# Expert rows added to the token rows in memory by accumulating scatters, and the last norm added to x1 in the output by accumulating stores

## The chip, the cores and the metric

The kernel runs on one core of one Trainium2 chip. The metric is device time in microseconds (us); lower is better. The core has a matrix engine (TensorE, PE in the profile), a vector engine (VectorE, DVE), a scalar engine (ScalarE, ACT), a general engine (GpSimd, POOL) and a synchronising engine (SyncE, SP), each with an instruction stream of its own that runs strictly in order. SP and POOL issue nearly all transfers of this kernel. The transfers themselves run on 16 DMA engines, which all queues share. What SP issues shows up in the profile as queue q1 (hardware_dynamic), what POOL issues as queue q0 (software_dynamic).

## What is computed

A residual block of attention and a residual block of a feed-forward layer, each between two layer norms. 4096 tokens of 512 numbers, in float32. The feed-forward layer has one shared expert for all tokens and eight experts of which each token uses two.

```
def _moe_forward(hidden_states, ...):
    x = hidden_states.reshape(-1, h)
    shared = jnp.einsum('ti,hi->th', jax.nn.silu(x @ sh_gate_w.T) * (x @ sh_up_w.T), sh_down_w)
    probs = jax.nn.softmax((x @ router_weight.T).astype(jnp.float32), axis=-1)
    top_v, top_i = jax.lax.top_k(probs, TOP_K)
    top_v = top_v / top_v.sum(axis=-1, keepdims=True)
    combine = (jax.nn.one_hot(top_i, E, dtype=top_v.dtype) * top_v[..., None]).sum(axis=1)
    out = jnp.zeros_like(x)
    for e in range(E):
        gu = x @ gate_up_proj[e].T
        gate, up = (gu[:, :I_MOE], gu[:, I_MOE:])
        cur = jax.nn.silu(gate) * up @ down_proj[e].T
        out = out + cur * combine[:, e:e + 1]
    return out + jax.nn.sigmoid(x @ shared_gate_w.T) * shared
...
x = x + _layernorm(_L0_attn_ref(_layernorm(x, axis=-1), ...), axis=-1)
x = x + _layernorm(_L0_ffn_ref(_layernorm(x, axis=-1), ...), axis=-1)
```

The x after the first of the last two lines is called x1 below.

## The kernel before

Tokens go in 8 batches of 512 (4 chunks of 128 rows; 32 chunks in all). `schedule()` writes out one list of pieces by hand, and every engine runs those pieces of the list that it has a part in, in the order of the list. So the list sets what is queued behind what on each engine. Every product is made of three matrix instructions (high and low halves of both factors; `three`, lines 690 to 692).

There are three stages.

1. **Attention, with the shared expert of batches 0 to 6 between its pieces** (0 to about 1495 us). It computes x1, stores it to `x1_scratch` (piece `x1o`), routes the tokens and scatters each token's normed row to two places in `x1_normed_by_expert`, where rows stand sorted by expert in pages of 256 (piece `sc`, 8 indirect transfers per batch; it is filled with zeros first by piece `zf`, 13 transfers in the first batch). The shared expert's weights come in halves of 128x768 into three buffers `ffn_w_raw` (piece `raw`, L643), and its result, times its gate, goes to `shared_scratch` (piece `sho`).
2. **The experts** (1495 to about 2008 us). 39 pages of two halves, so 78 steps of 128 rows. In step j POOL fetches the page's weights by an indirect load (`rgu`, L572, 128x2816 numbers, two buffers; `rdn`, L579, 128x1536, one buffer), ACT and DVE split them into high and low parts (`WG`, `WD`), PE computes, ACT copies the result to `moe_y` (L1032) and SP stores it to `expert_out` (piece `yo`, L666).
3. **The end** (2008 us on). PE runs the shared expert for batch 7: 11 tiles (76 < n < 88) of 36 matrix instructions, 24 for gate and up and 12 for down. Beside it, chunk by chunk, the final sum and norm run: SP loads x1 and the shared rows (piece `fl`, L675 and L677, 8 buffers), POOL gathers the token's two expert rows from `expert_out` (L591), DVE adds them by weight (L1317, two per chunk) and takes statistics (`FA`, L1320), DVE computes the norm's factors for four chunks (`FR`, a chain of 12 small operations), ACT shifts x1 and DVE adds the normed row (`FX`, L1039 and L1333), and SP stores the output (piece `fo`, L681). The load for chunk q+8 waits until the store of chunk q has landed (line 674), because it uses the same buffer.

In stage 3 the gate of tile n+1 waits on PE for the DVE product of tile n (`SI`, L1282) and for the split weights of its own tile (`SPL`, L1272 and L1275); the down product waits for `HL` (L1285).

Of the kernel before, what the change touches and what calls it, by code (L numbers as in the profile page):

```python
# [50 lines left out]
XG = 3  # L51
FS = 8
# [116 lines left out]
def moe_step(j):  # L169
# [36 lines left out]
def final_chunk(q):  # L206
    return [("FX", q), ("fo", q)] + ([("fl", q + FS)] if q + FS < NCH else [])

# [9 lines left out]
def schedule():  # L218
# [21 lines left out]
    for n in range(INTERLEAVED, F_MOE):  # L240
# [6 lines left out]
        if k == 8:  # L247
            parts[2] += [("XT", 0), ("xg", 3), ("rgu", 2)]
# [10 lines left out]
    for q in range(FS):  # L259
        seq += [("fl", q)]  # L260
    tiles = NF - F_MOE
    early = BEFORE * NC
# [5 lines left out]
    done_ = 0  # L268
    span = 3 * tiles - 6
    for i in range(3 * tiles):  # L270
        n = F_MOE + i // 3
        for p in ffn_parts(n)[i % 3]:
            if p[0] == "EV":
                seq += queue_rest(queue, done_)
                done_ = len(queue)
                seq += [("EV", *p[1:]), ("FA", NC * p[1] + p[2])]
                if p[2] == NC - 1:
                    seq += [("FR", p[1])]
                    for c in range(NC):
                        seq += final_chunk(NC * p[1] + c)  # L280
            elif p[0] != "sho":
                seq += [p]
        upto = min(len(queue), (i + 1) * len(queue) // (NT * 3 - 3))
        for p in queue[done_:upto]:
            seq += p
        done_ = max(done_, upto)
    for p in ffn_last(NF - 1):
        if p[0] == "EV":
            seq += [p, ("FA", NC * p[1] + p[2])]
# [6 lines left out]

def queue_rest(queue, done_):
    return [p for ps in queue[done_:] for p in ps]
# [44 lines left out]
def build(nc, x, w_att, w_ffn, w_gu, w_dn, w_router, b_qk, b_v, b_out, t_mask, t_dq, t_dk, t_lam, t_blk, t_ident,  # L344
          t_rank, t_newton, t_route, out):
    x_d = x.rearrange("(b c p) d -> b c p d", b=NB, c=NC)
    out_d = out.rearrange("(n p) d -> n p d", p=P)
    x1_d = nc.dram_tensor("x1_scratch", [NCH, P, D], F32, kind="Internal").ap()
    xt_d = nc.dram_tensor("xt_scratch", [NB, 2, P, KT * TOK], F32, kind="Internal").ap()
    sh_d = nc.dram_tensor("shared_scratch", [NCH, P, D], F32, kind="Internal").ap()  # L350
# [1154 lines left out]
```

## Time and profile before

| | us |
|---|---|
| Median of three runs (2217.8 to 2221.76) | 2218.04 |
| The profiled execution, its own time | 2218.5 |
| Its span in the trace | 2216.5 |
| PE busy | 2000.0 |
| DVE busy | 1272.7 |
| ACT busy | 962.8 |
| POOL busy | 266.5 |
| DMA, mean over the span | 188 GB/s |

The profiled execution is 2.0 us longer than its span, and 0.5 us above the median. PE is busy for 90% of the span, but this share is not the same in all stages. The page's 40 slices show tenths of a slice of 55 us: PE stands at 9 from slice 4 to slice 36 and at 6, 5, 6 and 4 in the last four, and the clock granted to PE is 9 (nine tenths or more) through all of the middle and 8, 7, 8 and 7 in the last four. Those four slices are stage 3. The names that the trace prints drop digits: `x_scratch` is `x1_scratch`, `fin_x` is `fin_x1`, `x_normed_by_expert` is `x1_normed_by_expert`.

### The profile page before, as it was taken

The page shows a single profiled execution, that of the slowest core. Times are in us where ns is not written, and L with a number is a line of the kernel's source. Part 1 is how long each engine was busy: PE and PEld are TensorE (multiplying, and loading weights), DVE is VectorE, ACT ScalarE, POOL GpSimd, SP SyncE. Part 2 cuts the span into 40 slices and gives each one's busy share as a digit, 9 for nine tenths or more (in the row PEclk, how much of TensorE's full clock was granted, in tenths as well). Part 3 has the DMA queues.
Part 4 walks back from the last instruction along what each step waited for, and adds up shares of the span by engine and source line. Part 5 has one row for each costly group of instructions (what it writes and reads, how often), then busy time and mean ns, then how long its engine had stood idle before and what let it go on. Part 6 is the DMA issues. An engine that isn't in the chain of part 4 may idle for free.

```text
span 2216.5 us, 28811 instructions
## 1 busy us (share of the span) xinstructions
PE 2000.0 (90%) x10192; PEld 1602.9 (72%) x10192; DVE 1272.7 (57%) x2960; ACT 962.8 (43%) x1946; POOL 266.5 (12%) x310
## 2 busy tenths in 40 slices
PE   6787999999999999999999999999999999996564
PEld 4465677777677776776777677779999999995443
DVE  3545564655555655655755554446666666665676
ACT  4333343433443443443443343346666666662222
POOL 1101001001001001001001002011111111115330
PEclk9898999999999999999999999999999999998787
DMA  7966245454355256254454347357777777757773
GB/s 246 399 218 214 60 146 194 141 169 162 107 171 179 69 182 205 69 186 144 134 190 133 103 137 247 108 194 239 245 247 244 242 243 245 252 186 256 233 261 125
DMA packets 153663, 416.85 MB, mean 188 GB/s; under 512 B 18401, under 2 KB 18545, under 8 KB 146353
## 3 DMA queue, kind: packets, MB, share of 16 engines
q1 hardware_dynamic: 118656, 239.13, 33.7%
q0 software_dynamic: 34432, 175.80, 22.0%
q8 instruction: 83, 1.36, 0.3%
q14 instruction: 60, 0.48, 0.1%
q10 hardware_dynamic: 432, 0.07, 0.0%
HBM read 307.98 MB, written 106.95 MB: 187 GB/s over the span
## 4 chain that ended last, share of the span: by engine, by line
PE 76%; DVE 11%; DMA 6%; issue 3%; ACT 2%; SPq 1%; POOL 0%; DVEq 0%; ACTq 0%
PE banks L690 21%; PE banks L692 20%; PE banks L691 20%; PE banks L753 4%; DMA xT_lo<-xt_scratch 2%; DMA out<-fin_x 2%; PE banks L761 2%; PE banks L765 2%; PE banks L865 2%; DVE fin_shared L1317 1%; PE banks L771 1%; DMA ffn_w_raw<-w_ffn 1%; PE banks L871 1%; PE banks L719 1%; DVE pair_stats L1079 1%
## 5 line engine op out<-in xcount | busy, mean ns | idle before, releaser
L690 PE MATMUL banks<-xT_hi,ffn_gate_up_hi 128*128 128x512 f32 x704 | 307.4, 437 | 73.1 <-DVE hidden_late L1282 40.6
L691 PE MATMUL banks<-xT_lo,ffn_gate_up_hi 128*128 128x512 f32 x704 | 284.8, 404 | 0.0
L692 PE MATMUL banks<-xT_hi,ffn_gate_up_lo 128*128 128x512 f32 x704 | 284.7, 404 | 0.0
L690 PEld LDWEIGHTS banks<-xT_hi,ffn_gate_up_hi 128*128 128x128 f32 x704 | 138.4, 197 | 126.4 <-DVE hidden_late L1282 53.5
L690 PE MATMUL banks<-moe_gu_hi,moe_xT_hi 128*128 128x352 f32 x624 | 215.7, 346 | 3.4 <-DVE moe_xT_lo L1299 3.4
L940 ACT COPY q_one_head<-qT 32x128 f32<-32x128 f32 x512 | 151.1, 295 | 117.8 <-PE banks L753 112.5
L692 PE MATMUL banks<-moe_gu_hi,moe_xT_lo 128*128 128x352 f32 x624 | 201.8, 323 | 0.0
L691 PE MATMUL banks<-moe_gu_lo,moe_xT_hi 128*128 128x352 f32 x624 | 201.3, 323 | 0.0
L1292 DVE TENSOR_TENSOR moe_gu_lo<-moe_gu_raw,moe_gu_hi 128x704 fp32r<-128x704 f32 x156 | 135.1, 886 | 96.7 <-ACT moe_gu_hi L1006 96.7
L691 PEld LDWEIGHTS banks<-xT_lo,ffn_gate_up_hi 128*128 128x128 f32 x704 | 139.1, 198 | 32.4 <-issue 7.4
L692 PEld LDWEIGHTS banks<-xT_hi,ffn_gate_up_lo 128*128 128x128 f32 x704 | 138.0, 196 | 30.9
L1275 DVE TENSOR_TENSOR ffn_gate_up_lo<-ffn_w_raw,ffn_gate_up_hi 128x768 fp32r<-128x768 f32 (+1 forms) x176 | 120.8, 686 | 61.6 <-ACT ffn_gate_up_hi L970 61.4
L690 PE MATMUL banks<-ffn_down_hi,hidden_hi 128*128 128x512 f32 x308 | 132.9, 431 | 4.4 <-DVE hidden_lo L1285 4.4
L947 ACT CAST attT_hi<-banks 128x256 fp32r<-128x256 f32 x64 | 23.7, 370 | 256.3 <-PE banks L765 256.2
L753 PE MATMUL banks<-q_one_head,kT 128*128 128x512 f32 x256 | 132.5, 611 | 0.6 <-ACT q_one_head L940 0.6
L1141 DVE TENSOR_TENSOR probsT<-banks,decay_mask 128x512 f32<-128x512 f32 x128 | 87.4, 689 | 67.5 <-PE banks L753 65.6
L1296 DVE TENSOR_TENSOR moe_dn_lo<-moe_dn_raw,moe_dn_hi 128x512 fp32r<-128x512 f32 x117 | 77.2, 687 | 83.9 <-ACT moe_dn_hi L1012 83.9
L690 PEld LDWEIGHTS banks<-moe_gu_hi,moe_xT_hi 128*128 128x128 f32 x624 | 118.1, 189 | 7.3 <-DVE moe_xT_lo L1299 3.6
L691 PEld LDWEIGHTS banks<-moe_gu_lo,moe_xT_hi 128*128 128x128 f32 x624 | 119.2, 191 | 3.3
L692 PE MATMUL banks<-ffn_down_hi,hidden_lo 128*128 128x512 f32 x308 | 120.9, 392 | 0.0
L691 PE MATMUL banks<-ffn_down_lo,hidden_hi 128*128 128x512 f32 x308 | 120.5, 391 | 0.0
L1006 ACT CAST moe_gu_hi<-moe_gu_raw 128x704 fp32r<-128x704 f32 x156 | 118.6, 785 | 0.0
(233 smaller groups left out, 4283.1 us busy)
## 6 DMA issues: line engine op xcount, KB each, us to landing
ffn_w_raw<-w_ffn SPq DMA_DIRECT2D x176, 384.0 KB, 3.2
att_w_hi<-att_w_split SPq DMA_DIRECT2D x112, 256.0 KB, 3.7
att_w_lo<-att_w_split SPq DMA_DIRECT2D x112, 256.0 KB, 4.5
x_normed_by_expert<-xT_hi POOLq DMA_DIRECT2D x13, 1536.0 KB, 10.2
moe_x<-x_normed_by_expert SPq DMA_DIRECT2D x78, 256.0 KB, 3.0
expert_out<-moe_y SPq DMA_DIRECT2D x78, 256.0 KB, 2.9
x_in<-x SPq DMA_DIRECT2D x32, 256.0 KB, 4.7
x<-x SPq DMA_DIRECT2D x32, 256.0 KB, 5.3
```

The costliest lines, as they stand in the source:

```text
L690: pe.matmul(out_ap, l_hi, r_hi, start=start, stop=False)
L691: pe.matmul(out_ap, l_hi, r_lo, start=False, stop=False)
L692: return pe.matmul(out_ap, l_lo, r_hi, start=False, stop=stop)
L753: mm = pe.matmul(b, kT[:, g, c * P:(c + 1) * P], qz[:, g % 2].rearrange("p h t -> p (h t)"), start=True, stop=True)
L761: pe.matmul(b[:, cols], state[:, g, :], qd[:, g, :], start=(gl == 0), stop=False, skip_group_check=True)
L765: mm = pe.matmul(b[r, cols], v[:, c, g * P + j * HD:g * P + (j + 1) * HD], probs[:, g % 2, j, :], start=False, stop=(gl == 1), skip_group_ ...
L940: op = act.copy(qz[r, g % 2, j, :], qT[r, g, c * P:(c + 1) * P])
L1006: op = act.copy(gu_hi[:, i % 2, k, :], rgu[:, i % 2, k * GU:(k + 1) * GU])
L1141: op = ve.tensor_tensor(probs[:, g % 2, :, :], chunked(b), mask[:, GH * g:GH * (g + 1), :], ALU.mult)
L1275: op = ve.tensor_tensor(wgu_lo[:, n % WGU, gu_cut], src, wgu_hi[:, n % WGU, gu_cut].bitcast(F32), ALU.subtract)
L1292: op = ve.tensor_tensor(gu_lo[:, i % 2, k, :], rgu[:, i % 2, k * GU:(k + 1) * GU], gu_hi[:, i % 2, k, :].bitcast(F32), ALU.subtract)
L1296: op = ve.tensor_tensor(dn_lo[:, i % 2, k, :], rdn[:, k * D:(k + 1) * D], dn_hi[:, i % 2, k, :].bitcast(F32), ALU.subtract)
```

## The change

- The two expert rows of a token are no longer kept in `expert_out`. Each expert step scales its rows by the routing weight (ACT, now an activation with a scale) and POOL adds them with an accumulating scatter into `ffn_out`, one row per token, in which the shared expert's result of batches 0 to 6 already stands. Rows of batch 7 and 256 rows for unused places are set to zero in the first batch.
- So that a step knows weight and token of its rows, the rows of `x1_normed_by_expert` grow from 512 to 514 numbers (2048 to 2056 bytes): the weight in number 512, the token's id in 513. The eight scatters of a batch (`sc`) become four, a wait until they have landed, a POOL copy of the second weight, and four more. The zero fill writes 514-number rows in 26 transfers in place of 13, plus one for `ffn_out`.
- A scatter of page g waits until both scatters of page g-1 have landed. `moe_y` has 4 buffers in place of 2, `moe_x` 8 in place of 3; a load of `moe_x` waits for the scatter that used the buffer.
- x1 goes to the output itself. In stage 3 there is one load per chunk (`fl`, SP), no gather, one statistics operation on DVE (for batch 7 also one sum with the shared result out of the accumulators), one ACT operation for the norm, and one store from POOL that adds to the output (`fo`). Every chunk has its own buffer; only semaphores are shared by 16.
- The final pieces are dealt over all 33 parts of the 11 tiles from the fifth part on; before, over the first 27 or so.

```diff
@@ sizes
-XG = 3
-FS = 8
+XG = 8
+FW = 16
+LEAD = 8
+FINALS_FROM = 4
+DX = D + 2
+NY = 4
@@ moe_step: the load of moe_x comes after the scatter that it waits for
-            if j + 1 + XG < NJ:
-                out += [("xg", j + 1 + XG)]
...
         out += [("MD", j - 1), ("yo", j - 1)]
+        if j - 1 + XG < NJ:
+            out += [("xg", j - 1 + XG)]
@@ schedule: the end
     for b in range(BEFORE):
-        queue += [[("FA", NC * b + c)] for c in range(NC)]
+        for c in range(NC):
+            q = NC * b + c
+            queue += [([("fl", i) for i in range(LEAD + 1)] if q == 0 else [("fl", q + LEAD)] if q + LEAD < NCH else []) + [("FA", q)]]
         queue += [[("FR", b)]]
         queue += [final_chunk(NC * b + c) for c in range(NC)]
...
+    for i, part in enumerate(parts):
+        seq += [p for p in part if p[0] not in ("EV", "sho")]
+        upto = max(0, (i - FINALS_FROM + 1) * len(queue) // (len(parts) - FINALS_FROM))
+        for p in queue[given:upto]:
             seq += p
-        done_ = max(done_, upto)
+        given = max(given, upto)
@@ zero fill (POOL)
-               in_=zero.unsqueeze(1).to_broadcast([P, ZROWS // (2 * P), 2 * D])).then_inc(xs_zero, 16)
+                    tail = acc_d[(NB - 1) * TOK:, :].rearrange("(n p) d -> p n d", p=P)
+                    pool.dma_start(out=tail, in_=unused_row[0][:, 0:D].unsqueeze(1).to_broadcast([P, NC + SUB, D])).then_inc(acc_zero, 16)
+                rows = xs_d[i * ZROWS:(i + 1) * ZROWS, :].rearrange("(n s p) d -> s p n d", p=P, s=SUB)
+                for k in range(SUB):
+                    pool.dma_start(out=rows[k], in_=unused_row[k].unsqueeze(1).to_broadcast([P, ZROWS // GT, DX])
+                                   ).then_inc(xs_zero, 16)
@@ sc (POOL)
+                    if k == 0:
+                        for c in range(NC):
+                            pool.wait_ge(xs_out[c], 32 * a + 16)
+                        pool.tensor_copy(xn2[:, :, D], cw2[:, :]).then_inc(second_weight, 1)
+                        pool.wait_ge(second_weight, a + 1)
@@ yo: from SP to POOL
-                sp.dma_start(out=y_d[j * P:(j + 1) * P, :], in_=y[:, j % 2, :]).then_inc(y_out[j % 2], 16)
+                if j >= SUB:
+                    for i in range(SUB):
+                        pool.wait_ge(y_out[i], 16 * (j // SUB))
...
+                pool.indirect_dma_start(
+                    out=acc_d[:, :], out_offset=bass.IndirectOffsetOnAxis(ap=xg[:, j % XG, D + 1:DX].bitcast(I32), axis=0),
+                    in_=y[:, j % NY, :], in_offset=None, compute_op=ALU.add).then_inc(y_out[j % SUB], 16)
@@ fl and fo
-                if q >= FS:
-                    sp.wait_ge(out_stored[q % FS], 16 * (q // FS))
-                sp.dma_start(out=fx1[:, q % FS, :], in_=x1_d[q]).then_inc(fin_in[q % FS], 16)
-                if q < BEFORE * NC:
-                    sp.dma_start(out=fsh[:, q % FS, :], in_=sh_d[q]).then_inc(fin_in[q % FS], 16)
-                sp.dma_start(out=out_d[q], in_=fx1[:, q % FS, :]).then_inc(out_stored[q % FS], 16)
+                if q >= FW:
+                    sp.wait_ge(v_piece, done("V", "FA", q - FW))
+                sp.dma_start(out=fsh[:, q, :], in_=acc_d[q * P:(q + 1) * P, :]).then_inc(fin_in[q % FW], 16)
...
+                pool.dma_start(out=out_d[q], in_=fsh[:, q, :], accum_op=ALU.add).then_inc(out_stored[q % FW], 16)
@@ FA (DVE)
-                for k in range(2):
-                    chain(ve, ve.scalar_tensor_tensor(out=fsh[:, i % FS, :], in0=fy[:, i % FS, k, :],
-                                                      scalar=cw[k][:, i:i + 1], in1=fsh[:, i % FS, :], op0=ALU.mult,
-                                                      op1=ALU.add))
+                if b >= BEFORE:
+                    ve.wait_ge(p_piece, done("P", "DN", NF - 1))
+                    chain(ve, ve.scalar_tensor_tensor(out=fsh[:, i, :], in0=acc[:, c, :], scalar=sig[:, i:i + 1],
+                                                      in1=fsh[:, i, :], op0=ALU.mult, op1=ALU.add))
@@ MD (ACT)
-                op = act.copy(y[:, i % 2, :], mout[i % 2])
+                op = act.activation(y[:, i % NY, :], mout[i % 2], ACT.Copy, scale=xg[:, i % XG, D:D + 1])
```

How this moves instructions, on SP in stage 3. In the kernel before, the waits for a landed store (`out_stored`) stand between the weight loads (L643):

```order
L643 DMA ffn_w_raw<-w_ffn 128x768 [waits dve_piece] x2
L681 DMA out<-fin_x1 128x512 [waits dve_piece]
L675 DMA fin_x1<-x1_scratch 128x512 [waits out_stored4]
L677 DMA fin_shared<-shared_scratch 128x512
L681 DMA out<-fin_x1 128x512 [waits dve_piece]
L675 DMA fin_x1<-x1_scratch 128x512 [waits out_stored5]
L677 DMA fin_shared<-shared_scratch 128x512
L681 DMA out<-fin_x1 128x512 [waits dve_piece]
```

In the changed kernel the same stretch of SP holds only weight loads and loads of `ffn_out`:

```order
L671 DMA fin_ffn_out<-ffn_out 128x512 x3
L643 DMA ffn_w_raw<-w_ffn 128x768 x2
L671 DMA fin_ffn_out<-ffn_out 128x512
L643 DMA ffn_w_raw<-w_ffn 128x768
L671 DMA fin_ffn_out<-ffn_out 128x512 x3
L643 DMA ffn_w_raw<-w_ffn 128x768 x2
```

The stores have moved to POOL, and with them every wait on a transfer. On POOL in stage 2 the kernel before has only weight fetches, each of which waits for DVE:

```order
L572 DMA moe_gu_raw<-w_gu,w_index 128x2816 [waits dve_piece]
L579 DMA moe_dn_raw<-w_dn,w_index 128x1536 [waits dve_piece]
L572 DMA moe_gu_raw<-w_gu,w_index 128x2816 [waits dve_piece]
L579 DMA moe_dn_raw<-w_dn,w_index 128x1536 [waits dve_piece]
L572 DMA moe_gu_raw<-w_gu,w_index 128x2816 [waits dve_piece]
```

In the changed kernel a scatter stands before each of them, and each scatter carries a wait for the landing of earlier ones (`moe_y_added`):

```order
L586 DMA ffn_out<-moe_y,moe_x 4352x512 [waits moe_y_added1,moe_y_added0,act_piece]
L573 DMA moe_dn_raw<-w_dn,w_index 128x1536 [waits dve_piece]
L586 DMA ffn_out<-moe_y,moe_x 4352x512 [waits moe_y_added1,moe_y_added0,act_piece]
L566 DMA moe_gu_raw<-w_gu,w_index 128x2816 [waits dve_piece]
L586 DMA ffn_out<-moe_y,moe_x 4352x512 [waits moe_y_added1,moe_y_added0,act_piece]
```

So a weight fetch is now queued behind a wait on the transfer of the step before.

## Rows read from the trace of the kernel before

**Rows 1.** Busy time by stretch: us, engines (instructions), PE clock, DMA share, GB/s.
```profile
core 0: us, PE busy (x) PEld busy (x) DVE busy (x) ACT busy (x) POOL busy (x), PEclk, DMA share, GB/s
50.00:120.00 70.00, 54.90 (x297) 35.27 (x298) 41.87 (x99) 26.03 (x76) 10.28 (x15) 0.90 1.02 390
1495.00:2008.00 513.00, 511.68 (x3047) 478.11 (x3046) 314.39 (x489) 313.06 (x566) 67.86 (x72) 1.00 0.69 233
2008.00:2197.00 189.00, 116.70 (x398) 87.97 (x396) 126.69 (x276) 46.92 (x81) 68.81 (x64) 0.81 0.75 248
```

**Rows 2.** Waits from 2008 to the end: who for whom, us, times, longest.
```profile
ACT ffn_gate_up_hi L967 <- DMA ffn_w_raw<-w_ffn: 41.2, 5, 12.0
...
PE banks L690 <- DVE hidden_late L1282: 40.6, 7, 12.6
...
PE banks L690 <- DVE hidden_lo_late L1285: 23.2, 9, 3.6
```

**Rows 3.** The chain of waits, 2138 to 2170: start, us, what.
```profile
2141.57 7.33 DMA out<-fin_x
...
2153.98 5.84 DMA out<-fin_x
...
2161.04 6.21 DMA ffn_w_raw<-w_ffn
```

**Rows 4.** Timeline of PE: first of three instructions, in stage 1 and stage 3.
```profile
1318.41 0.40 PE L690 MATMUL banks<-xT_hi,ffn_gate_up_hi 128*128 128x512 f32 x1
...
1333.38 0.39 PE L690 MATMUL banks<-ffn_down_hi,hidden_hi 128*128 128x512 f32 x1
...
2008.14 0.40 PE L690 MATMUL banks<-xT_hi,ffn_gate_up_hi 128*128 128x512 f32 x1
```

**Rows 5.** Transfers from 2008 to 2197: packets, MB, share; issues with median landing.
```profile
q1 hardware_dynamic: 15264, 30.02, 47.8%
q0 software_dynamic: 5120, 16.78, 26.7%
...
ffn_w_raw<-w_ffn SPq DMA_DIRECT2D x17, 384.0 KB, 6.1
```

**Rows 6.** Groups of instructions from 1980 on, by form: DVE's weighted sums.
```profile
L1317 DVE SCALAR_TENSOR_TENSOR fin_shared<-fin_y,combine,fin_shared 128x512 f32<-128x512 f32 x64 | 47.8, 746 | 14.5 <-DMA fin_y<-expert_out,pos_int 9.5 <-ACT fin_shared L998 3.9
```

**Rows 7.** The chain of waits from 2197 to the end.
```profile
2198.14 0.76 DVE fin_shared L1317
...
2206.22 0.70 DVE fin_stats L1320
...
2209.80 0.73 ACT fin_x L1039
...
2212.63 0.66 DVEq L357
```

**Rows 8.** Timeline of one page of stage 2: start, us, engine, instruction.
```profile
1707.91 0.53 DVE L1305 TENSOR_TENSOR moe_hidden<-banks,moe_silu 128x352 f32<-128x352 f32 x1 [0.45 <-ACT moe_silu L1027]
...
1710.27 0.49 PE L871 MATMUL banks<-identity,moe_hidden 128*128 128x128 f32 x3
...
1712.20 0.94 POOL L579 DMA_INDIRECT moe_dn_raw<-w_dn,w_index  x1 [5.20 <-DVE moe_dn_lo L1296]
...
1719.40 0.62 ACT L1012 CAST moe_dn_hi<-moe_dn_raw 128x512 fp32r<-128x512 f32 x1
```

**Rows 9.** Issues of stage 2 (1500 to 1950), with the median us to landing.
```profile
moe_dn_raw<-w_dn,w_index POOLq DMA_INDIRECT x33, 6.3
```

**Rows 10.** Issues of stage 1 (100 to 1400): the plain scatters.
```profile
x_normed_by_expert<-x_normed,pos_int POOLq DMA_INDIRECT x64, 3.0
```

**Rows 11.** POOL's queue from 50 to 125: packets, MB, share of 16 engines.
```profile
q0 software_dynamic: 5360, 20.97, 70.3%
```

**Rows 12.** Timeline of POOL: first work after the zero fill, and after a batch's scatters.
```profile
143.56 1.09 POOL L542 DMA_DIRECT2D x_scratch<-x  x2 [29.91 <-DVE x_shift L1073]
...
872.64 1.14 POOL L561 DMA_DIRECT2D shared_scratch<-shared_staged  x2 [12.29 <-ACT shared_staged L998]
```

More of the change, by code:

```diff
@@ L247, in schedule @@
         if k == 8:
-            parts[2] += [("XT", 0), ("xg", 3), ("rgu", 2)]
+            parts[2] += [("XT", 0), *(("xg", j) for j in range(3, XG)), ("rgu", 2)]
         if k in (7, 8, 9):
@@ L258, in schedule @@
         seq += moe_step(j)
[L259 to L262, printed above, removed]
     queue = []
     for b in range(BEFORE):
-        queue += [[("FA", NC * b + c)] for c in range(NC)]
+        for c in range(NC):
+            q = NC * b + c
+            queue += [([("fl", i) for i in range(LEAD + 1)] if q == 0 else [("fl", q + LEAD)] if q + LEAD < NCH else []) + [("FA", q)]]
         queue += [[("FR", b)]]
         queue += [final_chunk(NC * b + c) for c in range(NC)]
[L268 to L284, printed above, removed]
+    parts = [part for n in range(F_MOE, NF) for part in ffn_parts(n)]
+    given = 0
+    for i, part in enumerate(parts):
+        seq += [p for p in part if p[0] not in ("EV", "sho")]
+        upto = max(0, (i - FINALS_FROM + 1) * len(queue) // (len(parts) - FINALS_FROM))
+        for p in queue[given:upto]:
             seq += p
-        done_ = max(done_, upto)
+        given = max(given, upto)
     for p in ffn_last(NF - 1):
         if p[0] == "EV":
-            seq += [p, ("FA", NC * p[1] + p[2])]
+            seq += [("FA", NC * p[1] + p[2])]
         elif p[0] != "sho":
@@ L370, in build @@
         oh = [sb(f"one_hot{k}", [NCH, E]) for k in range(2)]
-        cw = [sb(f"combine{k}", [NCH]) for k in range(2)]
+        cw2 = sb("combine_second", [NC])
+        ids = sb("token_id", [NCH + SUB], I32)
         sig = sb("shared_gate", [NCH])
@@ L379, in build @@
         xt_lo = sb("xT_lo", [KT, TOK], F32R)
-        zero = xt_hi[:, 0:2, :].rearrange("p k t -> p (k t)").bitcast(F32)
         raw = sb("ffn_w_raw", [RAW, UNIT])
@@ L452, in build @@
         past = sb("page_past", [NG, E], scope=phase1)
-        rw_raw = xn2[:, NC - 1, 0:RWW]
+        rw_raw = xn2[:, 1, 0:RWW]
+        unused_row = [xn2[:, 2 + i, :] for i in range(SUB)]
         raw_flat = raw[:, :, :].rearrange("p r u -> p (r u)")
@@ L1195, in dve_attention @@
                 chain(ve, ve.reciprocal(sm["rs"][:, :, :], sm["s"][:, :, :]))
-                for k, m in enumerate(("m1", "m2")):
-                    chain(ve, ve.tensor_tensor(cw[k][:, blk4], sm[m][:, :, 0], sm["rs"][:, :, 0], ALU.mult))
+                ve.tensor_copy(xn2[:, :, D + 1].bitcast(I32), ids[:, blk4])
+                ve.tensor_tensor(xn2[:, :, D], sm["m1"][:, :, 0], sm["rs"][:, :, 0], ALU.mult)
+                chain(ve, ve.tensor_tensor(cw2[:, :], sm["m2"][:, :, 0], sm["rs"][:, :, 0], ALU.mult))
                 chain(ve, ve.tensor_scalar(sm["s"][:, :, :], sm["z"][:, :, :], 1.0, None, ALU.add))
@@ L1329, in dve_final @@
                                              op0=ALU.mult, op1=ALU.mult)
-            else:
-                b, c = divmod(i, NC)
-                ve.wait_ge(a_piece, done("A", "FX", i))
-                op = ve.scalar_tensor_tensor(out=fx1[:, i % FS, :], in0=fsh[:, i % FS, :], scalar=frstd[:, b % 2, c:c + 1],
-                                             in1=fx1[:, i % FS, :], op0=ALU.mult, op1=ALU.add)
             op.then_inc(v_piece, 1)
@@ L1347, in _ @@
                 sp_piece(sp, *p)
-            for i in range(FS):
-                sp.wait_ge(out_stored[i], 16 * (NCH // FS))
+            for i in range(FW):
+                sp.wait_ge(out_stored[i], 16 * (NCH // FW))
         @block.gpsimd
         def _(pool):
-            pool.memset(zero, 0.0).then_inc(const_p, 1)
+            for i in range(SUB):
+                pool.memset(unused_row[i], 0.0).then_inc(const_p, 1)
             pool.dma_start(out=rw_raw, in_=w_router).then_inc(late_in, 16)
@@ L1411, in _ @@
                     ve.wait_ge(late_in, 16 * N_LATE)
+                    ve.wait_ge(const_p, SUB)
+                    for i in range(SUB):
+                        ve.tensor_copy(unused_row[i][:, D + 1:DX].bitcast(I32), ids[:, NCH + i:NCH + i + 1]).then_inc(unused_id, 1)
                 elif p == ("L", 0, 0):
```

129 lines of the change are left out of this document (53 added, 76 removed), and 4 rows, old and new, of the table PARTS.

## The prediction

> **What bounds the kernel now.** I read busy time by stretch first. Stage 2 (1495 to 2008) has PE busy 511.7 of 513 us at a granted clock of 1.00: only PE's own work sets it [rows 1]. Stage 3 is different: in 189 us PE is busy 116.7, at a granted clock of 0.81, so it spends time between the levels of 1.2 and 2.4 GHz [rows 1]. It idles 72.3 us. The waits say for whom: 40.6 for the DVE product of the last tile and 23.2 for the low half of the hidden rows [rows 2]. Both stand in DVE's in-order stream behind something else. ACT in turn waits 41.2 us for weight halves [rows 2]. The chain of waits shows why these are late: a store lands after 7.33 us, another after 5.84, and only then SP issues the weight load, which takes 6.21 more [rows 3]. The weight load itself is not slow; it stands on SP behind loads that wait for landed stores. At the start of the stage DVE likewise stands before the weighted sums until the first gathers are in.
>
> What PE could do there: in stage 1, where it is fed, 22 groups of three instructions take 1333.38 - 1318.41 = 14.97 us [rows 4], 0.68 a group. Stage 3 has 11 x 12 = 132 groups, 89.8 us, against 189.
>
> **Stage 3 after the change.** No instruction on SP waits for a store any more, DVE loses 64 sums of 746 ns (47.8 us) [rows 6] and the 32 last additions, and everything between the tiles becomes optional work.
>
> - PE. Gate and up of the first tile start at 2008.14 [rows 4] and last 8 groups, 5.4 us. The second tile's gate waits for one DVE product, about 0.8: 2014.4. Then 124 groups, 84.4 us, with one gap of 1.4 before the last down product (ACT and DVE split the last hidden rows while PE has nothing else; about two DVE-sized operations of 0.7): last matrix instruction at about 2100.2. Before: just before the first sum at 2198.14 less one ACT operation, about 2197.4 [rows 7].
> - DVE has 126.7 us busy in the stage [rows 1]. Less 47.8, less about 22 for the last additions, it is some 57 of 92 us, plus gaps within the factor chains (2.9 us each, from 2206.9 to 2209.8 [rows 7]). The longest chain in front of the product of a tile is 2.9, and PE has the four groups of the down product (2.7 us) as cover, so I charge nothing. Clock: with PE fed it was 1.00 in stage 2 [rows 1]; I take full speed. If it stayed at 0.81, 90 us would be 111.
> - The tail. Before, 2197.4 to 2216.5, 19.1 us. The sums: four chunks in 2198.14 to 2206.9, 2.2 us each with two sums; now one sum each and no ACT eviction ahead: 4 x 1.4 = 5.6. Factors 2.9, ACT 0.7 + 3 x 0.62 = 2.6, one issue 0.5, landing. The last store before was issued at the end of the row at 2212.63 (2213.3) and landed within 3.2 [rows 7]. I take 3.5 for a store that also adds. Sum 15.2, so the span would end at 2115.4.
>
> **The adding transfers** are what no row shows. Price by bytes: in stage 3, 30.02 MB took 47.8% of 189 us, 16.78 MB took 26.7% [rows 5], both 3.0 us per MB (all 16 engines). A store that adds must read its target and write it. The lower bound is a plain transfer (3.0 per MB). Two plain rows one after the other, one that reads memory and one that writes it, give 6.0, and that is the row pair nearest to it: I take 6.0. The upper bound I set at 12, because a read of the same bytes that has to come back before each write may not overlap anything; nothing excludes it. A gain below a plain store is excluded, since the same bytes are written.
>
> Stage 3 then moves 8.4 MB of `ffn_out` loads, 6.7 of weights (17 x 0.393) and 8.4 of adding stores: 15.1 x 3.0 + 8.4 x 6.0 = 96 us of DMA time. The first load waits for the last scatter, about 2015, so until 2115 there are 100 us. That is 95% use, against 75% before, when weights landed in 6.1 us [rows 5]. A weight half may take until three halves later (3 x 4.1 us, less 1.5 for the splits). Some will be late: I charge 6 us, and 2 for DVE standing at the first statistics. With 3.0 per MB both are nothing.
>
> The Trainium skill has this price too: Collectives: The Full Stack, "The bandwidth ceiling: the fold count and why AG ≠ RS ≠ AR", says a reducing transfer has two source reads and one write, and runs at half the rate of a copy. No run before shows it; by it the sum is what I took.
>
> **Stage 2.** A step lasts 513 / 78 = 6.6 us, in which DMA is busy 69%, 4.6 us [rows 1]. A scatter that adds costs 0.262 MB x 3.0 = 0.8 more: 82%. The thin place is the down weights, with one buffer: fetch at 1712.20, landing 6.3 [rows 9], so 1718.5, use at 1719.40 [rows 8]: 0.9 us spare. Behind that the product at 1707.91 to 1708.44 is used by PE at 1710.27: 1.8 spare [rows 8]. What is queued on POOL in front of this fetch is now a scatter that waits for the landing of one issued a step (6.6 us) earlier. About 1 us lies between its place and the fetch. So a scatter may take 6.6 + 1 + 0.9 + 1.8, about 10.3 us, before PE feels it. Plain scatters land in 3.0 [rows 10]; twice that is far inside. ACT's scaled copy has over a third of the step idle [rows 1] to hide in. Charge: 2 us, for weights that land later at 82% use. The deeper `moe_x` ring is loaded seven steps ahead.
>
> **Stage 1.** The wait inside `sc` puts about 5 us on POOL per batch (landing 3.0, a copy, the second weight); the shortest time that POOL then idles before its next work is 12.3 us [rows 12], so nothing. The zero fill is not free: from 50 to 120 us DMA is at 102% [rows 1]. 20.97 MB took 70.3% of 75 us, 2.5 us per MB at 4096-byte rows [rows 11]; at 2056-byte rows I take the 3.0 of stage 3, and 1.6 MB more are filled: 22.1 x 3.0 - 52.7 = 13.6 us more DMA time. The fill is through by about 120 before, by 134 after; what waits for it on ACT belongs to the x1 rows that POOL stores at 143.6 [rows 12]. What it may delay are the first weight loads of the second batch. Bounds 0 and 13.6, taken 2.
>
> **Sum.** 2115.4 + 6 + 2 + 2 + 2 = 2127.4 span, plus 2.0 outside it, less 0.5 for the median: about **2129** us, 4.0% less.
>
> **The rivals.**
> 1. *Adding costs more than twice* (chance 0.12). With 9 per MB stage 3 has 121 us of DMA time, and ends near 2140; stage 2 stands at 94% and the down weights are late by perhaps 0.5 us a page, 39 x 0.5 = 20: 2160. With 12 per MB stage 2 needs 4.6 + 2.4 = 7.0 of 6.6 us (+31) and stage 3 147: 2197. For it: two reads that must meet. Against: nothing yet.
> 2. *Slower than before: the scatter chain* (0.05). Each page's scatter waits for the landing of the last, and the weight fetch waits behind it. Above 10.3 us of landing every further us costs one per page. It takes (2218 - 2129 + 4) / 39 = 2.4 us more, so from about 12.7 us the kernel is slower, and at 15 us it ends at 2129 + 39 x 4.7 = 2312. For it: a gather or fetch from memory lands in 6.3 already. Against: 12.7 is four times the 3.0 of a plain scatter.
> 3. *The change does not do what it says: PE stays unfed* (0.07). The final loads stand on SP between the weight loads and wait for statistics on DVE, so half the idle time and the low clock may remain: 2115 + 50 + 12 = 2177.
> 4. *The padded rows* (0.06). Rows of 2056 bytes start anywhere. If they cost half as much again as 2048, the fill lasts until 150 and holds up ACT, and the 8 x 8 scatters and 78 loads weigh more: about +15, 2144. 
>
> **How the numbers follow.** The forecast (adding at 3 to 6 per MB, 2114 to 2142) has 0.70. Range: from all charges at nothing and a landing of 2.4 to the first rival's 9 per MB and the fourth: 2114 to 2165; it leaves out the third, the second, and the upper end of the first, about 0.19. A measurement here tells 0.2% (4.4 us) from no change. Faster by more: all but the second and a sliver of the first, 0.93; the same 0.02; slower 0.05.
>
> **What the changed profile would show.** Right: PE at 9 tenths or more and a clock near 1.0 from 2015 to 2100; waits of ACT for `ffn_w_raw` small; the landing of the adding scatter 4 to 8 us; share per MB of POOL's queue about twice that of SP's in stage 3; stage 2 at 513 to 516 us. Wrong: PE waits in stage 2 for the low half of the down weights, with POOL's scatters waiting for scatters; a scatter landing above 10 us; weight loads still landing after 8 us or more while PE idles in stage 3; or the first batch's end later than before by over 10 us.

## The result, and the profile after

The changed kernel takes 2146.71 us (median of 4 runs, 2140.51 to 2150.83) against 2219.9 for the kernel before beside it: a ratio of 0.967, 95% interval 0.964 to 0.970, so 3.3% faster. Forecast were 2129 us, 4.0%, a band of 2114 to 2142 with a chance of 0.70, and a range of 2114 to 2165: the time lies in the range, but above the band. The profiled run took 2150.83 us, with a span of 2149.0.

Busy time by stretch, the kernel after (columns as in [rows 1]): the fill, stage 2, stage 3 up to the last down product, the end.

```profile
50.00:120.00 70.00, 55.09 (x295) 35.86 (x296) 41.04 (x97) 25.63 (x75) 21.25 (x29) 0.88 1.03 352
1508.00:2021.00 513.00, 511.59 (x3050) 478.25 (x3049) 312.82 (x489) 319.30 (x566) 198.00 (x149) 1.00 0.86 231
2021.00:2127.00 106.00, 95.11 (x397) 75.52 (x395) 65.84 (x192) 49.07 (x81) 26.15 (x29) 0.97 0.88 214
2127.00:2149.00 22.00, 0.00 (x0) 0.00 (x0) 7.82 (x24) 2.93 (x4) 3.52 (x4) 0.55 0.37 55
```

Against [rows 1], stage 2 is as long as before and starts 13 us later. The whole gain is in stage 3 (83 us there, of which the later start takes 13 and the longer end 3), where the same matrix instructions (397 and 398 recorded) need 106 us instead of 189. PE's idle time falls from 72.3 to 10.9 us, which is 61.4. Its busy time falls from 116.7 to 95.1, another 21.6, because the granted clock stands at 0.97 instead of 0.81: a fed PE works nearly always at 2.4 GHz. The end after the last down product grows from about 19 to 22 us.

Waits from 2021 to the end, the kernel after (who for whom, us in total, times, longest), to be read against [rows 2]:

```profile
ACT fin_ffn_out L1020 <- DVE fin_shift L1306: 48.5, 8, 13.8
...
PE banks L678 <- DVE hidden_lo_late L1267: 5.3, 2, 5.0
...
PE banks L678 <- DVE hidden_late L1264: 4.6, 3, 2.2
...
ACT ffn_gate_up_hi L958 <- DMA ffn_w_raw<-w_ffn: 0.6, 1, 0.6
```

PE waits 10 us for DVE where it was 64, and ACT no longer waits for weights. In the kernel before, two rows of the same view, from 2008 on, belong beside [rows 2]:

```profile
ACT fin_x L1039 <- DVE fin_shift L1328: 82.4, 8, 21.8
...
ACT ffn_gate_up_hi L970 <- DMA ffn_w_raw<-w_ffn: 18.2, 3, 7.4
```

So ACT's waits for weights were 41.2 and 18.2 us, now 0.6. And ACT's longest wait, before its normalisations and for DVE's factors, is not new: it was 82.4 us and is 48.5. The prediction did not name this row.

Transfers from 2021 to 2127, the kernel after (columns as in [rows 5]):

```profile
q0 software_dynamic: 4156, 7.58, 47.2%
q1 hardware_dynamic: 7056, 15.08, 40.1%
...
out<-fin_ffn_out POOLq DMA_DIRECT2D x28, 256.0 KB, 6.7
ffn_w_raw<-w_ffn SPq DMA_DIRECT2D x17, 384.0 KB, 5.6
```

POOL's queue took 0.472 x 106 / 7.58 = 6.6 us per MB, SP's, all plain loads, 2.8. Weights still land in 5.6 us, although the engines are 88% used.

### The profile page after: what moved, and what is told of

Its sections match the earlier page's. It is cut to its first block, busy times and chain, and to the rows that moved or that the text cites. A ratio compares the mean times of both kernels' runs of the same rounds, so it can differ in the third digit from the quotient of the medians.

```text
span 2149.0 us, 28704 instructions
## 1 busy us (share of the span) xinstructions
PE 1991.3 (93%) x10192; PEld 1596.2 (74%) x10192; DVE 1204.6 (56%) x2878; ACT 969.1 (45%) x1942; POOL 370.3 (17%) x380
## 4 chain that ended last, share of the span: by engine, by line
PE 81%; DVE 7%; issue 4%; DMA 3%; ACT 2%; SPq 1%; POOL 1%; POOLq 0%; ACTq 0%; DVEq 0%
PE banks L678 23%; PE banks L680 22%; PE banks L679 22%; PE banks L741 4%; DMA xT_lo<-xt_scratch 2%; PE banks L749 2%; PE banks L753 2%; PE banks L853 2%; PE banks L759 1%; PE banks L859 1%; PE banks L707 1%; DVE probsT L1122 1%; DVE pair_stats L1060 1%; SPq L651 1%; POOL out L594 1%
## 5 line engine op out<-in xcount | busy, mean ns | idle before, releaser
L678 PE MATMUL banks<-xT_hi,ffn_gate_up_hi 128*128 128x512 f32 x704 | 303.0, 430 | 29.4 <-DMA xT_lo<-xt_scratch 22.0
L678 PEld LDWEIGHTS banks<-xT_hi,ffn_gate_up_hi 128*128 128x128 f32 x704 | 135.9, 193 | 80.6 <-issue 22.2
L586 POOL DMA_INDIRECT ffn_out<-moe_y,moe_x x78 | 125.3, 1607 | 282.8 <-ACT moe_y L1014 267.6
L531 POOL DMA_DIRECT2D out<-x x32 | 17.6, 553 | 610.1 <-DVE x_shift L1054 607.6
```

What stands on the lines that cost most here:

```text
L586: pool.indirect_dma_start(out=acc_d[:, :], out_offset=bass.IndirectOffsetOnAxis(ap=xg[:, j % XG, D + 1:DX].bitcast(I32), axis=0), in_=y[:, ...
L678: pe.matmul(out_ap, l_hi, r_hi, start=start, stop=False)
```

## The experiments

Beside each time stands the **last stretch** of its trace, from the last copy of an expert row on ACT to the end of the span. It leaves stages 1 and 2 out, and with them most of the scatter between runs. Ratios are to the kernel before on the same chip. Names with b_ are the kernel before with an edit, names with a_ the kernel after; "again" means no edit, and the other edits are shown below. The last stretch of one and the same kernel differs by 2 to 3 us between two traces (208.2 and 205.0, 127.9 and 125.5).

| kernel | us | ratio [95%] | last stretch |
|---|---|---|---|
| before (first trace) | 2219.9 | | 208.2 |
| b_again | 2223.1 | 1.000 [0.998, 1.002] | 205.0 |
| b_late_loads | 2195.0 | 0.987 [0.985, 0.989] | 175.2 |
| after (first trace) | 2146.7 | 0.967 [0.964, 0.970] | 127.9 |
| a_again | 2147.8 | 0.966 [0.964, 0.968] | 125.5 |
| a_plain_stores | 2143.7 | 0.963 [0.960, 0.965] | 124.1 |
| a_plain_scatters | 2146.2 | 0.965 [0.963, 0.967] | 129.0 |
| a_x1_loaded | 2147.4 | 0.966 [0.964, 0.968] | 129.8 |
| a_sp_back | 2148.1 | 0.967 [0.965, 0.969] | 131.7 |
| a_dve_back | 2208.7 | 0.994 [0.991, 0.996] | 192.8 |
| a_dve_back_late | 2190.1 | 0.987 [0.984, 0.990] | 175.4 |
| a_both_back | 2212.4 | 0.995 [0.993, 0.996] | 193.4 |
| a_late_norms | 2136.1 | 0.960 [0.958, 0.962] | 117.0 |
| a_late_split_end | 2126.7 | 0.956 [0.954, 0.958] | 107.4 |

**What the adding costs.** Two kernels overwrite where the kernel after adds.

```diff
-                pool.dma_start(out=out_d[q], in_=fsh[:, q, :], accum_op=ALU.add)
+                pool.dma_start(out=out_d[q], in_=fsh[:, q, :])
```

> The kernel after, with the stores of stage 3 overwriting the output rows instead of adding to them, so x1 is left out of the result. Theory (the adding costs the last stores their landing, and little before them): in the kernel after q0 took 58 us of engine time for 8.78 MB in stage 3, and the end ran from the last down products to the last byte in 21.9 us. With plain stores the four issues on POOL fall from 0.88 to about 0.54 us and the last landing from about 9 to 3.5 to 6 us, so the end shortens by 3 to 6 us and the whole is 2141 to 2144. Rival (the adding stores slow the weights and the first products by contention): the share of the DMA engines falls and 8 us or more come off, 2139 or less, with TensorE waiting clearly less than 10.8 us between 2021 and the last down product.

Measured: last stretch 124.1 against 125.5 and 127.9; 2143.7 us. PE waits as much as before (10.3 us for 10.8), so the rival falls. The issue of the last four stores takes 0.54 us each instead of 0.88, and the median landing of all 32 is 2.7 us instead of 6.5.

```diff
-                    in_=y[:, j % NY, :], in_offset=None, compute_op=ALU.add)
+                    in_=y[:, j % NY, :], in_offset=None)
```

> The kernel after, with the expert rows overwriting the token's row instead of being added to it, so sums over shared part and experts are left out. Theory (stage 2 stands on TensorE and hides what the adding costs): the issue on POOL falls from 1.59 to about 0.96 us, the landing from 5.4 to about 3, the DMA share of stage 2 from 0.86 to about 0.70, and the time moves by 3 us at most, 2144 to 2149. Rival (the adding is what the lower clock or the late first step of stage 2 comes from): stage 2 starts or runs 5 us or more earlier, 2140 or less.

Measured: no difference in time. Stage 2, this kernel, then POOL's queue in 440 us of stage 2 (1520 to 1960), in this kernel and in the kernel after:

```profile
1501.00:2013.00 512.00, 510.59 (x3044) 477.34 (x3043) 311.76 (x489) 316.79 (x566) 147.09 (x149) 1.00 0.64 232
```
```profile
q0 software_dynamic: 14718, 90.49, 54.9%
```
```profile
q0 software_dynamic: 18857, 90.50, 77.1%
```

For the same bytes the adding queue is busy 22.2% of 440 us, 97.7 us, longer. That is for 66 scatters of 0.262 MB: 5.6 us per MB more than a plain one. What a plain scatter alone costs no row shows; this queue's mean without adding is 0.549 x 440 / 90.49 = 2.7, and stage 3 had 3.0. With either as an estimate, adding costs about three times as much, 8.3 to 8.6 us per MB. PE idles 1.4 us of stage 2 either way (510.6 busy of 512, and 511.6 of 513): the price is paid from idle DMA time.

**One part undone.**

```diff
-    return [("FX", q), ("fo", q)]
+    return [("FX", q), ("FB", q), ("fo", q)]
+                sp.dma_start(out=fx1[:, q % FW, :], in_=out_d[q]).then_inc(fx1_in[q % FW], 16)
+                op = ve.tensor_tensor(fx1[:, i % FW, :], fx1[:, i % FW, :], fsh[:, i, :], ALU.add)
-                pool.dma_start(out=out_d[q], in_=fsh[:, q, :], accum_op=ALU.add)
+                pool.dma_start(out=out_d[q], in_=fx1[:, q % FW, :])
```

> The kernel after with only the second part of the change undone: x1 is loaded by SP (8 MB more on q1) and added on DVE by one pass a chunk (32 of 0.68 us), and the stores are plain; the adding scatters of stage 2 stay. Theory (DVE's passes set stage 3 above some 100 us of DVE work there): DVE goes from 74 to 96 us, the adding stores' landing leaves the end (3 to 5 us less there), and the time is 2150 to 2162, so that the adding stores are worth 3 to 15 us of the change and the scatters the rest. Rival (the adding stores cost as much as the pass that they save): within 3 us of after's 2147.7, or less.

Measured: 2147.4 us, 2 to 4 us more in the last stretch. The theory is wrong here: 21 us of further passes on DVE and 8 MB more to load cost about what the adding stores cost at the end. The second half of the change is worth nothing that these runs can tell. So the gain belongs to the first half and to what came with it, the dealing over all 33 parts and a buffer for every chunk. That is by exclusion: no kernel here undoes the first half with its gathers, or the dealing alone.

**SP's wait or DVE's work?** In the kernel before, one edit takes the refills from behind their own stores:

```diff
-    return [("FX", q), ("fo", q)] + ([("fl", q + FS)] if q + FS < NCH else [])
+    return [("FX", q), ("fo", q)]
-        queue += [[("FA", NC * b + c)] for c in range(NC)]
+        queue += [([("fl", NC * (b - 1) + c + FS)] if b and NC * (b - 1) + c + FS < NCH else []) + [("FA", NC * b + c)] for c in range(NC)]
```

> The kernel before, with one edit: a chunk's slot is loaded again not directly behind its own store but four chunks later, so that SP does not stand in front of the weight loads until a store has landed. Nothing is added in memory. Theory (stage 3 of before was slow because each refill waited some 6 to 7 us on SP for the store just issued, 24 times, and the weights queued behind it): ACT's 41 us of waiting for ffn_w_raw mostly go, stage 3 falls from 208 us to 120 to 150, and the whole to 2130 to 2160, which is the gain of the change without its adding. Rival (it is the traffic, the gathers and DVE's two sums a chunk that hold stage 3, which only the change removes): 2185 or more, with TensorE waiting on DVE or on landings instead.

Measured: 2195.0 us. It fits the rival better: 31 us off the last stretch, not 80. The stretches of b_late_loads (columns as in [rows 1]) and its waits on ACT and PE from 2018 on show what came in the place:

```profile
2050.00:2070.00 20.00, 13.49 (x43) 10.25 (x44) 18.46 (x40) 7.51 (x13) 10.20 (x10) 0.81 1.02 384
2070.00:2090.00 20.00, 16.00 (x64) 12.45 (x63) 18.42 (x42) 6.45 (x11) 8.69 (x8) 0.93 0.95 335
2090.00:2110.00 20.00, 15.01 (x54) 11.13 (x53) 18.36 (x40) 6.56 (x12) 8.48 (x8) 0.83 0.93 313
```
```profile
ACT fin_x L1039 <- DVE fin_shift L1328: 64.5, 6, 21.5
```
```profile
PE banks L690 <- DVE hidden_late L1282: 22.3, 5, 12.3
PE banks L690 <- DVE hidden_lo_late L1285: 19.7, 7, 5.0
```

DVE is busy 92%, and PE waits 42.0 us for it and 5.5 for anything else. But the DMA engines are full as well, so a further kernel loads DVE alone. It is the kernel after with three passes added in each chunk:

```diff
+                for k in range(3 if b < BEFORE else 2):
+                    chain(ve, ve.scalar_tensor_tensor(out=fsh[:, i, :], in0=fsh[:, i, :], scalar=ones[:, 0:1],
+                                                      in1=fsh[:, i, :], op0=ALU.mult, op1=ALU.max))
```

> The kernel after, with DVE's work of stage 3 put back: in each chunk three further passes over its 512 columns (two in the last batch) that leave the values as they are, 92 instructions of about 0.75 us, 69 us, in place of the 64 sums and 32 products that the change removes. Loads, adding stores and orders stay those of after. Theory (in b_late_loads DVE was 91 to 96% busy from 2050 to 2150, so what the adding in memory brought is that these passes left DVE): stage 3 grows by 35 to 50 us, the whole is 2180 to 2195, near b_late_loads' 2195, and TensorE waits for hidden_late and hidden_lo_late 30 us or more. Rival (b_late_loads was held by its 48 MB and the gathers, which fill the DMA engines to 0.95 to 1.0): DVE has room for these passes, and the time is 2165 or less.

Measured: 2208.7 us, 61 more than a_again; four fifths of the gain is gone, more than either side expected, and with DMA at only 0.6 to 0.7. (The shares are those of stretches of 20 us up to 2140.) The passes are not quite those of the kernel before: there one of the three stood behind the norm, here all three stand before the statistics, so the factors come later. The waits of a_dve_back on ACT and PE from 2017 on:

```profile
ACT fin_ffn_out L1020 <- DVE fin_shift L1309: 99.0, 8, 20.8
ACT hidden_late L966 <- DVE hidden_lo_late L1267: 14.9, 3, 7.6
```
```profile
PE banks L678 <- DVE hidden_lo_late L1267: 37.2, 6, 9.8
PE banks L678 <- DVE hidden_late L1264: 13.7, 5, 6.4
```

SP's wait put back alone:

```diff
-    return [("FX", q), ("fo", q)]
+    return [("FX", q), ("fo", q)] + ([("fl", q + LEAD)] if q + LEAD < NCH else [])
-                if q >= FW:
-                    sp.wait_ge(v_piece, done("V", "FA", q - FW))
+                if q >= LEAD:
+                    sp.wait_ge(out_stored[(q - LEAD) % FW], 16 * ((q - LEAD) // FW + 1))
```

> The kernel after, with SP's wait of before put back and nothing else: the load of a chunk's sums stands on SP directly behind the store of the chunk eight earlier and waits until that store has landed; the weight loads queue behind it. Theory (the wait on SP and DVE's passes are two costs, and each is worth something alone; taking the wait out of before gave 30 us, with DVE at 91 to 96% then): some 10 us a batch on SP, six times, so ACT waits 10 to 30 us for ffn_w_raw again and the time is 2160 to 2180. Rival (with DVE light there is room, and the loads land in time in spite of the wait): 2152 or less.

Measured: 2148.1 us; the rival holds. The last stretch, 131.7, is 4 to 6 us longer than in the two traces of after, so the wait may cost a few us, but not ten. SP does wait in this kernel, and ACT pays little. The waits on ACT and on SP from 2015 on:

```profile
ACT ffn_gate_up_hi L958 <- DMA ffn_w_raw<-w_ffn: 4.3, 5, 1.5
ACT ffn_gate_up_hi L961 <- DMA ffn_w_raw<-w_ffn: 2.0, 2, 1.2
```
```profile
SPq L671 <- DMA out<-fin_ffn_out: 62.6, 24, 8.2
```

In the kernel before, the same row reads:

```profile
SPq L675 <- DMA out<-fin_x: 116.7, 24, 8.5
```

The two edits together:

> The kernel after with both costs put back: DVE's 92 passes of a_dve_back and SP's wait for landed stores of a_sp_back. From the last expert row in ACT to the end, the traces so far have 127 us for after (mean of two), 132 with SP's wait, 193 with DVE's passes, and 175 and 207 for the kernel before without and with its SP wait. Theory (SP's wait costs only where DVE is loaded, since then a late weight half cannot be caught up): clearly more than the sum of the parts, 205 to 220 us for this stretch, and a time of 2222 to 2238. Rival (the two are independent, so SP's wait adds its 5 us again, and the 30 us in the kernel before came from its stores standing on SP too): 195 to 200 us for the stretch, 2208 to 2215 in all.

Measured: a last stretch of 193.4, against 192.8 with DVE's passes alone. The theory of an interaction falls; SP's wait of this kind costs nothing that can be told even beside a loaded DVE. So b_late_loads' 31 us need what these kernels do not have. At least two things differ: in the kernel before the stores stand on SP too, so a store is only issued when the one before it has landed (116.7 us of waiting, not 62.6), and it moves more than twice the bytes. Which of them it is was not separated.

**ACT in order.** The norms of a batch are placed one batch later, each behind the statistics of the next batch's chunk:

```diff
-[("fl", q + LEAD)] if q + LEAD < NCH else []) + [("FA", q)]]
+[("fl", q + LEAD)] if q + LEAD < NCH else []) + [("FA", q)] + (final_chunk(q - NC) if b else [])]
         queue += [[("FR", b)]]
-        queue += [final_chunk(NC * b + c) for c in range(NC)]
...
+        elif p[0] == "HH":
+            seq += [p] + [x for c in range(NC) for x in final_chunk(NC * (NB - 2) + c)]
```

> The kernel after, with the four normalisations and stores of a batch placed one batch later in stage 3, each behind the statistics of the next batch's chunk, and those of batch 6 behind the last tile's hidden cast. Theory (ACT works in order, so a normalisation that waits for DVE's factors holds up the hidden casts and silus that TensorE needs): ACT's 48.5 us of waiting for fin_shift fall below 20, TensorE's waits in stage 3 from 10.8 to 5 us or less, and 4 to 8 us come off, 2139 to 2143. Rival (the weights or DVE's own queue are late, whatever ACT does): TensorE waits as long as before and the time stays within 2 us of the kernel after.

Measured: 2136.1 us, 117.0 in the last stretch, 10 less: more than the theory's 4 to 8. PE's waits fall from 10.8 to 3.6 us. ACT's wait for the factors falls from 48.5 to 32.6 only, not below 20; the rest of it held nothing up that PE needed. The timeline of ACT in the kernel after, then in a_late_norms, shows the place (start, us, what):

```profile
2112.14 0.60 ACT L966 ACTIVATE hidden_late<-banks 128x512 f32<-128x512 f32 x1 [2.42 <-PE banks L680]
2118.31 2.93 ACT L1020 ACTIVATE fin_ffn_out<-fin_ffn_out,fin_shift,fin_rstd 128x512 f32<-128x512 f32 x4 [5.57 <-DVE fin_shift L1306]
2121.14 0.60 ACT L971 CAST hidden_hi_late<-hidden_late 128x512 fp32r<-128x512 f32 x1
```
```profile
2105.70 0.62 ACT L972 CAST hidden_hi_late<-hidden_late 128x512 fp32r<-128x512 f32 x1 [2.61 <-PE banks L681]
2107.70 2.93 ACT L1021 ACTIVATE fin_ffn_out<-fin_ffn_out,fin_shift,fin_rstd 128x512 f32<-128x512 f32 x4 [1.38 <-DVE fin_shift L1307]
```

In the kernel after, the last hidden cast stands behind four norms that stand behind the factors. It is done 9 us after its silu, and PE stands 5.0 of these. In a_late_norms the cast goes first.

> a_dve_back with the late order of a_late_norms: the same 92 added passes on DVE, but a batch's norms one batch later. a_dve_back took 2208.7 us, 61 more than after, with ACT waiting 99 us for fin_shift. Theory (DVE's 139 us of work are the bound, wherever ACT's norms stand): 2185 to 2203. Rival (the 61 us came from ACT, which waited in order for the late factors while hidden casts and silus stood behind): the late order takes most of it back, 2170 or less.

Measured: 2190.1 us, as the theory has it. The late order takes 18.6 us off a_dve_back and 11 off the kernel after. Between two kernels that both have the late order, a_dve_back_late and a_late_norms, the passes still cost 54 us (58 of the last stretch). So the load on DVE is the cause in either order, and ACT's order makes it some 7 us dearer.

**A shorter end.** On top of a_late_norms, the last batch is summed chunk by chunk while PE still works, and x1 is added on DVE:

```diff
+        seq += [("FX", q), ("FB", q), ("fs", q)]
-                    ve.wait_ge(p_piece, done("P", "DN", NF - 1))
+                    if c + 1 < NC:
+                        ve.wait_ge(last_down, c + 1)
+                    else:
+                        ve.wait_ge(p_piece, done("P", "DN", NF - 1))
+                sp.dma_start(out=out_d[q], in_=fx1[:, q % NC, :]).then_inc(last_out, 16)
```

> a_late_norms with another end: each chunk of the last batch is summed as soon as its own down products are done, not after all four; x1 of these four chunks is loaded ahead, added on DVE, and stored by SP without adding. Theory (the end after the last down product is a chain of sums 5.6, factors 2.9, norms 2.9, adding stores of 0.88 each on POOL and their landing of 6 to 9 us): 3.5 us come off the sums and 4 to 6 off the stores and their landing, 7 to 9 in all, so 2127 to 2130. Rival (the landing is bound by what is still queued, not by adding, and the extra pass and loads eat the rest): 2133 or more.

Measured: 2126.7 us, 9.4 less than a_late_norms and 4.4% less than the kernel before: the fastest of all. The last stores on SP, with their landing:

```profile
L687 SPq DMA_DIRECT2D out<-fin_x x4: 332/338/343, 2123.8 to 2125.9; - x4
```

The last is issued at 2126.2, its landing takes 2.1 us, and the span ends at 2128.4.

Three things changed here at once: the sums start earlier (DVE waits 1.8 us for PE before the first of them, 4.7 in a_late_norms), the last four stores do not add, and SP issues them, not POOL. The traces can tell the last apart. In the four in which SP issues the last store (before, b_again, b_late_loads, a_late_split_end) the last 0.75 us of the span move no byte, read in steps of 0.25; in the ten in which POOL issues it, the last 3.5 us move none, and plain stores on POOL (a_plain_stores, a_x1_loaded) do not change that. So nearly 3 of the 9.4 us go with the queue, not with adding. No kernel changes the queue alone.

**Stage 1.** Both kernels unchanged, once more:

> The kernel after, unchanged, once more beside the kernel before, to see how much of stage 1 belongs to the change. In the first pair of traces the first expert row left at 1495.4 us before and at 1509.1 after; in the trace of b_late_loads, whose stages 1 and 2 are those of before, it left at 1503.3, and in three variants of after at 1506.7, 1500.5 and 1504.4. Theory (what the change adds in stage 1 is small, and the rest of the 13.7 us is the granted clock, which differs from run to run): here the expert rows of after begin at 1500 to 1509 and those of the kernel before (b_again) at 1495 to 1504, with the same waits of TensorE as in the first pair, and the difference between the two is 2 to 7 us. Rival (the change itself costs stage 1 its 12 us): a difference of 10 us or more.

> The kernel before, unchanged, with a second trace. Theory (clock of the run): its first expert row leaves at 1498 to 1506 us, later than the 1495.4 of the first trace, and TensorE's waits in stage 1 are the same to 2 us. Rival (the change's own cost): it leaves at 1495 to 1497 again. The ratio against the kernel before is 1.00 either way.

Measured: the first and last copy of an expert row on ACT, in the traces of before, b_again, after and a_again:

```profile
L1032 ACT COPY moe_y<-banks x78: 585/586/588, 1494.8 to 2008.3; 128x512 f32<-128x512 f32 x78
```
```profile
L1032 ACT COPY moe_y<-banks x78: 585/587/588, 1499.1 to 2012.7; 128x512 f32<-128x512 f32 x78
```
```profile
L1014 ACT ACTIVATE moe_y<-banks,moe_x x78: 687/689/691, 1508.1 to 2021.1; 128x512 f32<-128x512 f32 x78
```
```profile
L1014 ACT ACTIVATE moe_y<-banks,moe_x x78: 687/689/689, 1503.5 to 2016.5; 128x512 f32<-128x512 f32 x78
```

A difference of 4.4 us here, 13.3 in the first pair. Over all traces the three with the stage 1 of before begin stage 2 at 1499.1 on average (1494.8 to 1503.3), the eleven with that of after at 1504.0 (1498.4 to 1509.7). So the change costs stage 1 about 5 us, with a standard error of some 3: with three traces of one kind it is not shown to cost anything, but the rival's 10 or more is not borne out either. The rest is the run. PE's waits between 100 and 1495 us are much the same in all of them (86 to 94 us); the delay is in its pace. The first scatters start 1 us later on average (196.3 and 197.3), so the fill is not the place. What makes the other 4, if they are there, stays open.

## Why the prediction was right, and where it was not

The direction, the size and the mechanism in outline hold: stage 2 is untouched, stage 3 runs nearly on PE's work at full clock (0.97, 10.9 us idle), and the adding is hidden. The time is 18 us above the forecast, outside the band of 2114 to 2142, and some terms that fit do so by chance. The upper part of the range, in which it lies, was made of dearer adding and padded rows; neither is where the 18 us went.

- **PE's work in stage 3**: 132 groups of 0.68 us at full clock. Measured 95.1 us busy, 5 more than the 89.8. The step holds, and so does the price set on a clock that stays at 0.81 (21 us): PE's busy time fell by 21.6.
- **What bounds the kernel now**: the prediction read the chain of stores, refills and weights on SP first. That wait alone, put back, costs at most a few us (a_sp_back, a_both_back); taken out of the kernel before, it gives 31 of 80 us. DVE's passes alone, put back, cost 61, and 54 in the late order. DVE was busy 126.7 of 189 us [rows 1], which looks like room; it was the engine in whose stream the tiles' products stood, as [rows 2] said. The sum was unharmed, since the change removes both.
- **"The longest chain in front of the product is 2.9 and PE has 2.7 as cover, so I charge nothing"**: this step failed. It looked at DVE alone. ACT works in order too, and its norms wait for that chain with the hidden cast behind them: 10 us (a_late_norms). The view of waits that [rows 2] are taken from had it, as its largest row, 82.4 us of ACT for `fin_shift`; the prediction read only ACT's wait for weights there.
- **6 us for late weights and 2 for the first statistics**: neither exists. ACT waits 0.6 us for weights, DVE 1.9 for statistics, and plain stores do not shorten PE's waits. The two charges stood, by luck, nearly where the 10 us of ACT belong.
- **The adding transfers**: taken at 6.0 us per MB between 3 and 12. Measured 6.6 for stores and, by the difference, 8.3 to 8.6 for scatters, which is near the price of the first rival (9). What that rival made of the price did not come: stage 2 took 86% of the DMA engines (82% and 94% were worked out), because without the adding it stands at 64% (a_plain_scatters), where 69 were taken, and no down weight came late enough for PE to feel it. The scatters' landing of 5.4 us (7.8 at most) is far from the 10.3 that PE would feel, so the second rival had no ground. The rule of the Trainium skill on reducing transfers (Collectives: The Full Stack, "The bandwidth ceiling: the fold count and why AG ≠ RS ≠ AR"), two reads and a write at half the rate of a copy, is stated there for a collective's ring; carried over to these transfers it gives the right order and is too kind: these runs show 2.4 times (6.6 to 2.8) and about 3 times the time.
- **Stage 2, 2 us**: nothing was lost; 513 us both times.
- **The end, 15.2 us**: measured 21.9. Sums 5.6 and factors 2.9 are as taken (the terms of this sum add up to 15.1). The four stores take 0.88 us each on POOL, one after the other from 2136.66 to 2140.2, where one issue of 0.5 was counted, and from there to the end it is 8.8 us, where 3.5 was taken. The 3.5 came from a store that SP had issued. With plain stores on POOL the same piece is 5.5 us (2138.3 to 2143.8 in a_plain_stores), and with plain stores on SP 2.2; so of the 5.3 us missed there some 3.3 are the adding and 2.0 the queue. The term is 6.7 short, and the end of a_late_split_end gives it back.
- **Stage 1, 2 us**: 13 in the trace shown, about 5 on average. The fill, taken at 3.0 us per MB, took 2.9 (79.7% of 75 us for 20.65 MB). The trace of before on which the sum stands happened to be the quickest of three there. The fourth rival, padded rows, forecast 2144 by a fill that lasts longer; the time came near it, but the first scatter moved by 1 us only.

So the 21.6 us between the span of the sum (2127.4) and that of the trace (2149.0) are about +11 in stage 1 (8 of them the run, if the average of 5 is taken for the change), -2 in stage 2, +6 in stage 3 and +7 at the end.

## What to carry to other kernels

A share of 67% does not acquit an engine: ask whose stream the critical product stands in and how much optional work is in front of it, on each in-order engine on the way (here DVE, then ACT); moving 70 us of passes off DVE was worth 50 to 60. It is not the passes by their number: the 21 us of passes that a_x1_loaded puts behind the norms cost 2 to 4, or at most 8 with what its plain stores save at the end. Optional work that waits for another engine's short chain belongs one round later in the order. Adding in memory is cheap while DMA time is idle. At the very end its landing is on the path, and there the issuing engine counts as much as the adding.

## What the runs showed of the hardware

- An adding store or scatter from SBUF costs 2.4 to 3 times the DMA time of a plain transfer: 6.6 us per MB for stores where SP's plain loads take 2.8, and 5.6 more than plain for scattered rows, with 63 packets more for each scatter (18857 - 14718 for 66).
- It also costs its issuer more: POOL is busy 1.59 us with an adding scatter and 0.97 with a plain one, 0.88 and 0.54 for stores.
- The last 3.5 us of the span move no byte when POOL issued the last store, plain or adding (ten traces), and the last 0.75 when SP did (four).
- 62.6 us in which SP's queue stood still before loads cost at most a few us (a_sp_back).
- The same stage 1 varies by 9 to 11 us from run to run, with equal waits: more than many changes are worth. Stretches that begin behind it compare far better than whole times.
